# Turning the similarity matrices through DRAM instead of TensorE, in a two-layer graph kernel

## The reference, cut to what matters

```python
h = relu(layernorm(x))
z_l, z_g, v = h @ W_lang.T, h @ W_grav.T, h @ W_V.T
zn  = z_l / max(norm(z_l), 1e-8)
A_l = max(zn @ zn.T, 0) * not_eye
sq  = sum(z_g * z_g)
A_g = exp(-max(sq + sq.T - 2 * z_g @ z_g.T, 0) / (2 * sigma ** 2)) * not_eye
K_l, K_g = row_stochastic(A_l * adj), row_stochastic(A_g * adj)
x = x + ((w_l * K_l + (1 - w_l) * K_g) @ v) @ W_O.T
x = x + (adj * adj).T @ relu(layernorm(x)) + bias
```

## Time and profile before

| | |
|---|---|
| median of the runs | 1269.22 us (1269.11 to 1269.99) |
| the profiled execution's own time | 1269.61 us |
| its span in the trace | 1267.7 us |
| TensorE busy | 1241.2 us, 98% |
| TensorE weight loads | 1039.6 us, 82% |
| VectorE busy | 1058.5 us, 83% |
| ScalarE busy | 694.5 us, 55% |
| GpSimd busy | 574.7 us, 45% |
| mean share of the 16 DMA engines | 27.2% for SP's queue and 7.9% for ACT's |
| granted TensorE clock, mean | 0.996 |

### The profile page before, as it was taken

One profiled execution on the slowest core, in us unless ns is written; L12 is line 12 of the kernel. 1 busy time (PEld: TensorE's weight loads), 2 busy tenths in 40 slices (PEclk: granted clock), 3 DMA queues, 4 the chain that ended last, 5 costly groups with the idle time before them and its releaser, 6 DMA issues.

```text
span 1267.7 us, 22572 instructions
## 1 busy us (share of the span) xinstructions
PE 1241.2 (98%) x6324; PEld 1039.6 (82%) x6324; DVE 1058.5 (83%) x1826; ACT 694.5 (55%) x1324; POOL 574.7 (45%) x964
## 2 busy tenths in 40 slices
PE   7999999999999999999999999999999999999996
PEld 6878888888888888888888888888888888888884
DVE  5678888988888988888898888898888898888777
ACT  5346555456645456655446655546655545654543
POOL 1115553434554434554434555444555443455433
PEclk9999999999999999999999999999999999999998
DMA  6232424342333343333343232344242444243201
GB/s 243 34 72 81 106 54 95 99 108 81 102 71 78 99 108 87 95 79 70 99 108 97 86 93 56 99 108 103 79 108 49 99 101 108 79 103 69 47 34 66
DMA packets 308894, 112.55 MB, mean 89 GB/s; under 512 B 269840, under 2 KB 269968, under 8 KB 308880
## 3 DMA queue, kind: packets, MB, share of 16 engines
q1 hardware_dynamic: 177360, 95.78, 27.2%
q10 hardware_dynamic: 131520, 16.60, 7.9%
HBM read 46.20 MB, written 33.62 MB: 63 GB/s over the span
## 4 chain that ended last, share of the span: by engine, by line
PE 93%; DVE 4%; ACT 1%; issue 1%; DMA 1%; POOL 0%; SPq 0%; DVEq 0%; ACTq 0%
PE ring L866 75%; PE p_ps L866 15%; PE p_ps L939 2%; PE kt_ps L879 1%; DMA h2f<-in_L_gnn_W_grav 1%; DVE x_out L688 0%; DVE bn L568 0%; DVE y_lo L557 0%; ACT h L379 0%; DVE bn L637 0%; DVE x_ring L631 0%; DVE y_lo L784 0%; DVE deg L602 0%; DVE v_lo L784 0%; DVE hT_lo L557 0%
## 5 line engine op out<-in xcount | busy, mean ns | idle before, releaser
L301 POOL TENSOR_TENSOR x_out<-x_ring,bias_sb 128x512 f32<-128x512 f32 x128 | 162.8, 1295 | 499.9 <-DVE bn L637 499.9
L866 PE MATMUL ring<-hT_hi,Lw_hi 128*128 128x512 f32 x640 | 256.9, 401 | 4.9 <-DVE hT_lo L576 2.1
L406 ACT ACTIVATE y_hi<-ring 128x512 fp32r<-128x512 f32 x256 | 148.3, 592 | 206.5 <-PE ring L866 203.7
L866 PE MATMUL ring<-hT_hi,Lw_lo 128*128 128x512 f32 x640 | 250.6, 392 | 0.0
L866 PE MATMUL ring<-hT_lo,Lw_hi 128*128 128x512 f32 x640 | 250.2, 391 | 0.0
L866 PE MATMUL ring<-MT_hi,hT_hi 128*128 128x512 f32 x512 | 203.0, 396 | 0.0
L557 DVE TENSOR_TENSOR v_lo<-ring,v_hi 128x512 fp32r<-128x512 f32 x128 | 88.5, 692 | 136.8 <-ACT v_hi L442 136.8
L866 PE MATMUL ring<-MT_hi,hT_lo 128*128 128x512 f32 x512 | 200.0, 391 | 0.0
L866 PE MATMUL ring<-MT_lo,hT_hi 128*128 128x512 f32 x512 | 199.9, 390 | 0.0
L308 POOL TENSOR_TENSOR h_lo<-h2f,h_hi 128x512 fp32r<-128x512 f32 x124 | 158.0, 1296 | 84.8 <-ACT h_hi L476 84.8
L557 DVE TENSOR_TENSOR y_lo<-ring,y_hi 128x512 fp32r<-128x512 f32 x256 | 169.2, 680 | 28.4 <-ACT y_hi L406 28.3
(11 more groups left out here) (160 smaller groups left out, 2537.0 us busy)
## 6 DMA issues: line engine op xcount, KB each, us to landing
x_ring<-in_x SPq DMA_DIRECT2D x32, 1024.0 KB, 5.5
out<-x_out SPq DMA_DIRECT2D x128, 256.0 KB, 2.2
h_turned<-h SPq DMA_DIRECT2D x248, 64.0 KB, 2.1
h_turned<-h ACTq DMA_DIRECT2D x248, 64.0 KB, 2.1
rn_cols<-rn_dram SPq DMA_DIRECT2D x31, 256.0 KB, 3.9
x_ring<-in_L_gnn_W_lang SPq DMA_DIRECT2D x4, 256.0 KB, 5.6
h2f<-in_L_gnn_W_grav SPq DMA_DIRECT2D x1, 1024.0 KB, 9.2
chain<-in_L_gnn_W_O SPq DMA_DIRECT2D x1, 1024.0 KB, 13.0
```

The source lines that it names most:

```text
L301: pool.tensor_tensor(x_out[:, b], x_rows(g, b), bias_sb[:, :], ALU.add).then_inc(x2b_ready, 1)
L406: act.activation(y[0][:, a, :, l], bank(n).rearrange("p (b m) -> p b m", b=GB), ACT.Copy)\
L866: mm = pe.matmul(out, lhsT, rhs, start=(k == 0), stop=(k == len(terms) - 1))
```

## The change

TensorE no longer transposes P, except in the last iteration. In its place VectorE transposes the 32x32 blocks of P (`turn_p`, one instruction for the lang part, one for the grav part) from `P_sb` into `P_blocks`, which is the space `diag`; SP stores each part to DRAM (`store_p`) and fetches it in four transfers (`fetch_p`) to `P_turned`, which is the first half of `h`. `sum_s` is split in two instructions, one for each part, reads SBUF only, and stands behind the four `output`. GpSimd multiplies the spread norms by the mask (`mask_norms`) into the space that `P_blocks` leaves free, behind the four `h2_lo` and ahead of the next `norm1`; so VectorE's `similarities` is gone and `mask_l` multiplies by `rn_mask`. ScalarE's `exponentials` goes from the end of an iteration to behind the second `y_hi` copy of the next one, `normalize` one `y_hi` copy later, `shift` ahead of `h2_copy` 0 and 1. VectorE's `turn_blocks` goes one `y_lo` later, so behind `combine` and not ahead of it. SP stores P ahead of the norms and fetches its first part between storing and loading the norms.

```diff
+        P_blocks = diag.rearrange("p b l m -> p (b l m)").rearrange("p (l j b q) -> p l j b q", l=2, j=NQ, b=GB)
+        P_turned = h[:, 0:2].rearrange("p l (i e) -> p l i e", i=NQ)
+        rn_mask = diag.rearrange("p b l m -> p (b l m)")[:, 0:GB * P].rearrange("p (b m) -> p b m", b=GB)
+        p_dram = [nc.dram_tensor(f"p_dram_{l}", [P, NQ, GB * Q], F32).ap() for l in range(2)]
...
+            def store_p(g, l):
+                sp.wait_ge(p_blocks, 2 * g + l + 1)
+                sp.dma_start(p_dram[l], P_blocks[:, l].rearrange("p j b q -> p j (b q)")).then_inc(p_stored[l], 16)
+            def fetch_p(g, l):
+                sp.wait_ge(p_stored[l], 16 * g + 16)
+                for j in range(NQ):
+                    sp.dma_start(P_turned[j * Q:(j + 1) * Q, l], p_dram[l][:, j].rearrange("(i r) e -> r i e", r=Q))\
+                      .then_inc(p_turned[l], 16)
+            def spread_norms_turn_p(g):
+                store_p(g, 0)
+                store_p(g, 1)
                 sp.wait_ge(rn_step, RN_STEPS * g + 1)
                 sp.dma_start(rn_dram, rn[:, 0]).then_inc(rn_stored, 16)
+                fetch_p(g, 0)
                 sp.wait_ge(rn_stored, 16 * g + 16)
                 sp.dma_start(rn_cols[:, :, :], rn_dram.unsqueeze(0).to_broadcast([P, P, GB])).then_inc(rn_spread, 16)
+                fetch_p(g, 1)
...
+            def mask_norms(g):
+                pool.wait_ge(rn_spread, 16 * g + 16)
+                pool.wait_ge(p_stored[0], 16 * g + 16)
+                by_row = mask[:, :].unsqueeze(1).to_broadcast([P, GB, P])
+                pool.tensor_tensor(rn_mask, rn_cols[:, :, :].rearrange("p m b -> p b m"), by_row, ALU.mult)\
+                    .then_inc(rn_masked, 1)
...
+                if after:
+                    mask_norms(i)
...
+                        act.wait_ge(s_ready, 2 * g - 2)
...
+                        if before and n == 2:
+                            exponentials(i - 1)
-                        if after and 3 <= n < 5:
-                            normalize(i + 1, (n - 3) * GB // 2)
+                        if after and 4 <= n < 6:
+                            normalize(i + 1, (n - 4) * GB // 2)
...
+                    if b == 0 and after:
+                        shift(i)
                     if before and b == 0:
                         h2_copy(i - 1, 0)
                         h2_copy(i - 1, 1)
-                    if b == 0 and after:
-                        shift(i)
...
-                if after:
-                    exponentials(i)
...
             def mask_l(g):
-                dve.wait_ge(a_ready, 3 * g + 1)
+                dve.wait_ge(rn_masked, g + 1)
+                dve.wait_ge(s_ready, S_STEPS * (g + 1))
+                dve.scalar_tensor_tensor(out=A[:, :, 0], in0=A[:, :, 0], scalar=0.0,
+                                         in1=rn_mask,
+                                         op0=ALU.max, op1=ALU.mult).then_inc(a_ready, 1)
...
-                        if after and n == 4:
-                            turn_blocks(i + 1, 0)
-                            turn_blocks(i + 1, 1)
                         if before and n == 4:
                             combine(i - 1)
                         if after and n == 5:
+                            turn_blocks(i + 1, 0)
+                            turn_blocks(i + 1, 1)
+                        if after and n == 6:
                             turn_blocks(i + 1, 2)
                             turn_blocks(i + 1, 3)
...
                 squared_norms(i)
+                turn_p(i, 0)
                 for b in range(GB):
...
                     turned_lo(i + 1, b)
-                    if b == 2:
-                        sum_s(i)
+                    if b == 0:
+                        turn_p(i, 1)
                 if before:
                     for b in range(GB):
                         output(i - 1, b, n + b)
-                similarities(i)
+                sum_s(i, 1)
+                sum_s(i, 0)
                 mask_l(i)
...
+            def turn_p(g, l):
+                if l == 0:
+                    dve.wait_ge(sq_ready, 3 * g + 2)
+                    wait_for(dve, p_stored[1], 16 * g)
+                else:
+                    dve.wait_ge(p_shifted, g + 1)
+                dve.transpose(P_blocks[:, l].rearrange("p j b q -> p b j q"),
+                              P_sb[:, :, l].rearrange("p b (j q) -> p b j q", q=Q)).then_inc(p_blocks, 1)
+            def sum_s(g, l):
+                dve.wait_ge(p_turned[l], 16 * NQ * (g + 1))
+                turned_l = P_turned[:, l].rearrange("p i (b q) -> p b i q", b=GB)
+                dve.tensor_tensor(A[:, :, l].rearrange("p b (i q) -> p b i q", q=Q), turned_l,
+                                  P_sb[:, :, l].rearrange("p b (i q) -> p b i q", q=Q), ALU.add).then_inc(s_ready, 1)
...
-                    if b == (2 if after else 0):
+                    if b == 0 and not after:
                         pe.wait_ge(p_shifted, i + 1)
                         for k in range(2 * GB):
                             mm = pe.transpose(p_ps[:, k // 2, k % 2], P_sb[:, k // 2, k % 2], ident[:, :])
```

More of the change, by code:

```diff
@@ L30, in gnn_pair @@
     RN_STEPS = 2
+    S_STEPS = 2
     blk = {ac: n for n, ac in enumerate(TRI)}
@@ L165, in gnn_pair @@
         blocks_ready, turned = sem("blocks_ready"), sem("turned")
+        p_blocks = sem("p_blocks")
+        p_stored, p_turned = [[sem(f"p_{what}_{l}") for l in range(2)] for what in ("stored", "turned")]
         ht_hi, ht_lo = sem("ht_hi"), sem("ht_lo")
@@ L171, in gnn_pair @@
         diag_ready = sem("diag_ready")
-        rn_step = sem("rn_step")
+        rn_step, rn_masked, a_scaled = sem("rn_step"), sem("rn_masked"), sem("a_scaled")
         def passes(hi_lo_lhs, hi_lo_rhs):
@@ L209, in store_out @@
                                  x_out[:, b]).then_inc(out_stored, 16)
-            def spread_norms(g):
+            def store_p(g, l):
[9 more added lines that the diff above has]
+                store_p(g, 1)
                 sp.wait_ge(rn_step, RN_STEPS * g + 1)
                 sp.dma_start(rn_dram, rn[:, 0]).then_inc(rn_stored, 16)
+                fetch_p(g, 0)
                 sp.wait_ge(rn_stored, 16 * g + 16)
                 sp.dma_start(rn_cols[:, :, :], rn_dram.unsqueeze(0).to_broadcast([P, P, GB])).then_inc(rn_spread, 16)
+                fetch_p(g, 1)
             def turn_h(g):
@@ L227, in iteration @@
                 if after:
-                    spread_norms(i)
+                    spread_norms_turn_p(i)
                 store_out(i - 1, first_use(i) + PER - GB)
@@ L246, in _ @@
             turn_h(1)
-            spread_norms(0)
+            spread_norms_turn_p(0)
             sp.wait_ge(w_split, 3 * C)
@@ L425, in iteration @@
                 if before:
-                    act.wait_ge(s_ready, i)
-                    act.wait_ge(diag_ready, 2 * i)
+                    act.wait_ge(s_ready, 2 * i)
                 for half in range(2):
@@ L439, in iteration @@
                     if not after and b == 1:
-                        exponentials(i)
+                        exponentials(i, 2)
                     act.wait_ge(v_done, GB * i + b + 1)
@@ L482, in shift, with exponentials @@
                 e.then_inc(p_shifted, 1)
-            def exponentials(g):
-                act.wait_ge(s_ready, g + 1)
+            def exponentials(g, steps=1):
+                act.wait_ge(s_ready, 2 * g + steps)
                 act.activation(A[:, :, 1], A[:, :, 1], ACT.Exp, scale=inv_sig2).then_inc(exp_done, 1)
@@ L577, in turned_lo, with mask_l_last @@
                    .then_inc(ht_lo, 1)
[L579 to L586, removed]
             maskb = mask[:, :].unsqueeze(1).to_broadcast([P, GB, P])
             def mask_l(g):
-                dve.wait_ge(a_ready, 3 * g + 1)
+                dve.wait_ge(rn_masked, g + 1)
[3 more added lines that the diff above has]
+                                         op0=ALU.max, op1=ALU.mult).then_inc(a_ready, 1)
+            def mask_l_last(g):
+                dve.wait_ge(r_done, 1)
+                dve.wait_ge(s_ready, S_STEPS * (g + 1))
+                dve.tensor_tensor(A[:, :, 0], A[:, :, 0], r_ps[:, :, :], ALU.mult).then_inc(a_scaled, 1)
+                dve.wait_ge(a_scaled, 1)
                 dve.scalar_tensor_tensor(out=A[:, :, 0], in0=A[:, :, 0], scalar=0.0, in1=maskb,
@@ L600, in row_factors @@
             def row_factors(g):
-                dve.wait_ge(a_ready, 3 * g + 3)
+                dve.wait_ge(a_ready, 2 * g + 2)
                 dve.tensor_reduce(deg[:, 0], A, AX.X, ALU.add).then_inc(deg_step, 1)
@@ L738, in iteration, with sum_s_last @@
                         output(i - 1, b, n + b)
-                similarities(i)
+                sum_s(i, 1)
+                sum_s(i, 0)
                 mask_l(i)
-            def sum_s(g):
-                dve.wait_ge(pt_done, g + 1)
-                dve.tensor_tensor(A, p_ps[:, :, :, :], P_sb, ALU.add).then_inc(s_ready, 1)
```

(13 more changed lines are left out.)

## The result

The changed kernel takes 1283.09 us (median; 1281.96 to 1283.51) where the kernel before took 1269.61 in the same comparison: a ratio of 1.0105, with a 95% interval of 1.0093 to 1.0117. It is slower by 1%; 1281.5 was forecast.

What follows compares the result with a forecast made beforehand. Bound: the loop through GpSimd's `h2_lo`, held `hT_lo` and VectorE's list, not TensorE. Terms 0 + 0.2 + 0.2 + 0 = +0.4 us per round, 30 rounds +12 us, forecast 1281.5 us; 8-in-10 range 1258 to 1300.

Steps and rivals of the forecast that it cites:

- The loop named in the prediction: Each round: `k_v`, residual, factors, ScalarE's list, `h2_lo`, `hT_lo`, VectorE's list, `kt_lo`, `k_v`; TensorE's transposes outside, gain 0.
- Block transposes, `sum_s` in the v phase: VectorE's two `turn_p` stand in its waits, cost 0; `sum_s` leaving the v phase gains 0.
- VectorE's tail: VectorE behind the outputs, to the first `y_lo`: 1.90 us for 1.71, +0.2 per round, bounds +0.2 to +1.1.
- `combine`: With `turn_blocks` behind it, VectorE's `combine` waits for ScalarE's scaled K: +0.2 us per round.
- GpSimd and the lock: New SBUF meetings of `mask_norms`, `norm1` with VectorE's `sum_s`, `mask_l`: -0.1 to +0.6 us per round, taken as 0.
- The other moves: `exponentials` and `shift` moved in ScalarE's list: cost 0.
- the second rival: GpSimd's `norm1` ends late, delaying `normalize`, K, `combine`, `kt_lo`: 1299 us; room 0.3 to 1.2 us; chance 0.20.
- Transfers: SP's norms and P fetches land in time: cost 0, up to +1 if a fetch is twice as slow.
- The faster rival: `hT_lo` runs at 601.14 beside `h2_lo`, unheld: -0.37 us per round, 1258, or 1245 if all comes through; chance 0.15.

Runs made afterwards that it cites:

- the first experiment: Kernel before without the eight TensorE transposes of P in all rounds but the last, sum reading P itself: 1268.17 us, ratio 0.9985.

## Why the prediction was right

**The bound.** The loop named in the prediction is the one that was there. Removing the transposes alone moved the time by 0.15%, and the fourth `hT_lo` took up the saved time in its 1.53 us. Leaving out GpSimd's instruction brought `hT_lo` back to 0.68 us. These two and the order of ends (0.53 to 0.59 us behind GpSimd's in each run in which the fourth `hT_lo` was held) show the exclusion between the two engines. A late `v_hi` is ruled out as the cause by the first experiment, where it came sooner and changed nothing; a late `layer1` by the move of `output`, which left `layer1` where it was and shortened `hT_lo`.

**Block transposes, `sum_s` in the v phase:** forecast 0; measured 0.01 us per round for the transposes. `sum_s` was not tried by itself.

**VectorE's tail:** forecast +0.2; 612.39 - 610.47 = 1.92 us for 1.71 before, +0.21. The 32-element runs cost what rows cost: 1.27 for two sums.

**`combine`:** forecast +0.2; the stretch from the end of `row_factors` (616.34) to the end of `kt_lo` (623.59) is 7.25 us, and before it was 7.04. The mechanism is the one named. ScalarE's scaling of K ends at 616.37 + 1.28 = 617.65 and `combine` starts at 617.68, 1.34 us behind the end of `row_factors` (forecast 1.36); before, the block transposes started there at 1.15. So the wait is worth 0.19. But the experiment that undid the order gave back only 0.08, because a second delay lies under the same wait: the two `y_lo` start 0.06 behind the end of the row factors, where they had started 0.06 ahead of it. These 0.12 us stand in a usual round of every version of the changed kernel (without GpSimd's part they stand one instruction earlier), and the sum of the prediction has no such term. In the changed kernel they cost nothing, since `combine` waits for ScalarE anyway; with the block transposes in front again the stretch is 7.17 us and not 7.04. That the 0.2 needed no correction for it is luck. Why the `y_lo` start later stays open.

**GpSimd and the lock:** forecast 0, between -0.1 and +0.6; nothing is left over: 0.21 + 0.21 = 0.42 from the held `hT_lo` to `kt_lo` (15.44 us for 15.02), 0.02 less from `k_v` to the end of `hT_lo` and 0.01 less from `kt_lo` to `k_v` give the 0.39 of a round. 30 of them are 11.7 us; the spans differ by 12.5, and two longer rounds (38.37 and 38.42) make 0.5 of the rest. `norm1` did meet the sums, but there GpSimd was held and not VectorE: its small steps at 610.67 and 611.20 took 0.56 and 0.61 us for 0.23 and 0.20, and the two sums their plain 1.27. `mask_norms` was bounded by 1.27 and 2.0. It shows 2.02, but 1.55 where it starts alone, so about half a microsecond of it is its own wait behind `hT_lo`, and that the upper bound was met is luck. `normalize` waits 0.43 for GpSimd, which the 0.59 of ScalarE's later pause still covers. So the second rival was 0.6 us away, within the 0.3 to 1.2 that the prediction gave it, and a second such instruction costs 1.4 us and more.

**The other moves** (`exponentials`, `shift`): forecast 0. None was undone by itself; the sum above leaves nothing for them.

**Transfers:** forecast 0. In the changed kernel GpSimd waits for the norms in 14 regular rounds, 0.2 to 1.0 us each. Twelve of these rounds last their 38.13 to 38.17 all the same; the two with the longest waits, 0.83 and 1.03, are the two longer ones. Waits of up to 0.67 us were covered; when the rest is quicker, shorter ones count.

**The faster rival** had its condition wrong by one instruction: the interface is not to be had at 606.63, but another instruction of VectorE can be put there. Its price, 0.37 us per round less than before, was too large: with the interface free the usual short rounds of that experiment last 37.5, 0.2 less than before, and the mean of all its rounds, 37.93, is longer than before. With the first `output` moved and two more orders the route through DRAM does gain, 6.6 us, and not 11 or 24.5.

## What to carry to other kernels

An engine that is 98% busy and on the chain everywhere can still be outside the loop that sets the pace; look at what ends each of its short waits, and at instructions that last longer than their equals. Where VectorE and GpSimd both work from SBUF, list the pairs that may meet, and put VectorE instructions that read PSUM beside GpSimd's long ones. When work leaves the bounding engine for others, the order on those decides: the same added work cost 1% in one order and gained 0.6% in another. And two delays can lie under one wait: undoing one of them then shows less than it costs.

## What the hardware showed that I had not expected

Not each GpSimd instruction holds VectorE. In the changed kernel the first `hT_lo` (598.95, 0.68 us) ran its plain time beside GpSimd's power of four columns, which stood from 598.64 to 599.66; the kernel before shows the same pair at 593.42 and 593.09:

```profile
598.95 0.68 DVE L606 TENSOR_TENSOR hT_lo<-h_turned,hT_hi 128x512 fp32r<-128x512 f32 x1
```

```profile
598.64 1.02 POOL L342 TENSOR_TENSOR rn<-sqc,neg_half 128x4 f32<-128x4 f32 x1
```

The Trainium skill (SBUF — State Buffer, "SBUF: two separate sides") says that whoever starts first has the pair "for the whole instruction". For the subtractions of 512 columns the traces agree; for this one they do not, and the measurement decides. Why, no run shows.

With a stride of 16 bytes in one input GpSimd took 1.55 us for 1.27, and VectorE 1.07 for 0.69. The Trainium skill (GPSIMD Engine Reference, "Performance pitfalls for Q7 kernels") puts reads with a stride over 8 bytes at half as much again per element, for kernels written for GpSimd's own cores; this built-in instruction took a fifth more, with one of two inputs strided.
